# A selective scan in 64 units: two spread inflows, a shorter look-ahead for GpSimd, and a transposed output projection

## The reference

```
shift, scale, gate = split(silu(c) @ Wada.T + bada)
skip = ln(x) * (1 + scale) + shift          # then a second ln
act_mx = silu(Wx x_ssm + bx)
z_d = Wc_d (Wz x_ssm + bz) + bc_d           # d = 1 forward, d = 2 on the flipped sequence
delta, B, C = projections of z_d
h_t = exp(delta_t * A_n) * h_(t-1) + delta_t * B_t,n * z_t      # for each n of 16
y_t = sum_n h_t,n * C_t,n  (+ z_t * Dp)
out = Wf (act_mx*y1 + act_mx*y2) + bf + skip
return x + gate * out
```

## Time and profile before

| | us |
|---|---|
| median of 3 runs | 3407.84 (3405.9 to 3410.21) |
| profiled execution, its own time | 3410.34 |
| its span, first to last instruction | 3408.4 |
| mean granted TensorE clock | 0.965 of full |

### The profile page before, as it was taken

How to read it: one execution, slowest core, us unless ns; L and a number is a source line. 1 busy time by engine, 2 the same in 40 slices (tenths; PEclk the granted TensorE clock), 3 DMA queues, 4 the chain that set the end, 5 groups by cost and what they waited for, 6 DMA issues and landing times.

```text
span 3408.4 us, 49569 instructions
## 1 busy us (share of the span) xinstructions
PE 2982.9 (88%) x17232; PEld 2142.3 (63%) x17232; DVE 3090.2 (91%) x1983; ACT 2667.4 (78%) x5070; POOL 2982.0 (87%) x1352
## 2 busy tenths in 40 slices
PE   8987888898888888888888888898888888888898
PEld 3554666666666666666666666666666666666665
DVE  2546999999999999999999999999999999999995
ACT  0336898988788898987777898988777898987772
POOL 1335999999999999999999999999999999999996
PEclk9988999999999999999999999999999999999999
DMA  5575344744557344645457334645457344644463
GB/s 217 177 251 186 127 138 141 236 157 164 176 189 261 131 139 142 237 143 168 158 199 249 131 134 145 231 150 162 158 197 255 125 143 141 225 155 161 152 214 114
DMA packets 215920, 594.67 MB, mean 174 GB/s; under 512 B 21276, under 2 KB 67548, under 8 KB 211320
## 3 DMA queue, kind: packets, MB, share of 16 engines
q1 hardware_dynamic: 213224, 572.63, 49.7%
q0 software_dynamic: 2304, 16.78, 1.3%
q10 hardware_dynamic: 144, 2.10, 0.2%
HBM read 510.79 MB, written 80.63 MB: 174 GB/s over the span
## 4 chain that ended last, share of the span: by engine, by line
DVE 27%; PE 25%; POOL 21%; issue 17%; ACT 1%; DVEq 0%; POOLq 0%; ACTq 0%
POOL hbuf L1201 16%; DVE slot L1298 15%; DVE hbuf L1298 8%; PE y L868 7%; POOL bst L1196 5%; PE mb L950 4%; PE mb L839 3%; PE slot L879 3%; DVE hbuf L1303 2%; DVE delta L1240 2%; PE slot L890 2%; PE mb L849 1%; PE mb L941 1%; PE mb L909 1%; ACT abuf L1101 1%
## 5 line engine op out<-in xcount | busy, mean ns | idle before, releaser
L1201 POOL TENSOR_TENSOR hbuf<-hbuf,cres 128x1024 f32<-128x1024 f32 x640 | 1507.5, 2375 | 174.5 <-DVE hbuf L1298 173.7
L1196 POOL TENSOR_TENSOR bst<-bst,du 128x1024 f32<-128x1024 f32 x576 | 1359.3, 2376 | 62.5 <-DVE du L1250 60.9
L868 PE MATMUL y<-ident,hbuf 128*128 128x128 f32 x8192 | 1096.3, 282 | 86.7 <-POOL hbuf L1201 86.5
L868 PEld LDWEIGHTS y<-ident,hbuf 128*128 128x128 f32 x8192 | 968.5, 146 | 251.8 <-POOL hbuf L1201 165.3
L1298 DVE TENSOR_TENSOR_SCAN hbuf<-dec,slot 128x1024 f32<-128x1024 f32 x448 | 1019.5, 2276 | 80.9 <-PE slot L890 58.3
L1101 ACT ACTIVATE abuf<-dut,bt 128x128 f32<-128x128 f32 x3072 | 971.1, 387 | 0.0
L1298 DVE TENSOR_TENSOR_SCAN slot<-slot,bst 128x1024 f32<-128x1024 f32 x384 | 875.5, 2280 | 13.2 <-ACT slot L1160 12.6
L1160 ACT ACTIVATE slot<-delta,par 128x1024 f32<-128x1024 f32 x576 | 639.9, 1111 | 232.6 <-DVE hbuf L1303 212.7
L879 PE MATMUL slot<-ident,abuf 128*128 128x128 f32 x3072 | 426.1, 284 | 208.8 <-ACT abuf L1101 173.9
L1160 ACT ACTIVATE dec<-delta,par 128x1024 f32<-128x1024 f32 x448 | 510.9, 1140 | 96.0 <-DVE hbuf L1298 96.0
L879 PEld LDWEIGHTS slot<-ident,abuf 128*128 128x128 f32 x3072 | 356.4, 145 | 341.1 <-ACT abuf L1101 201.4
(11 more groups left out here) (152 smaller groups left out, 2207.1 us busy)
## 6 DMA issues: line engine op xcount, KB each, us to landing
bst<-bc_s SPq DMA_DIRECT2D x576, 512.0 KB, 3.8
cres<-bc_s SPq DMA_DIRECT2D x128, 512.0 KB, 7.0
wzs<-wz_s SPq DMA_DIRECT2D x64, 256.0 KB
yf_s<-yrd SPq DMA_DIRECT2D x32, 512.0 KB, 5.3
ybuf<-yf_s SPq DMA_DIRECT2D x32, 512.0 KB, 4.7
yg_s<-ybuf SPq DMA_DIRECT2D x31, 512.0 KB, 4.4
si_s<-silu SPq DMA_DIRECT2D x28, 512.0 KB, 6.0
silu<-si_s SPq DMA_DIRECT2D x28, 512.0 KB, 5.3
```

Source lines behind the costliest of these rows:

```text
L868: last = nc.tensor.matmul(y[:, j * P:(j + 1) * P], hbuf[:, q % HR, j * P:(j + 1) * P], ident[:], start=False, stop=(q % N == N - 1), is_tr ...
L1196: nc.gpsimd.tensor_tensor(bst[:, i % BR, :], bst[:, i % BR, :], du[:, k % 2, :], ALU.mult).then_inc(pool_b, 1)
L1201: nc.gpsimd.tensor_tensor(hbuf[:, q % HR, :], hbuf[:, q % HR, :], cres[:, q % N, :], ALU.mult).then_inc(pool_prod, 1)
```

## The change

- KINDS: chunk 1 becomes V, chunks 2 and 4 are E (before: E at 1, V at 2, A at 4). Six V, two E, five A, three P. A second diagonal tile, one made at c = 14, one at c = 0 of the next unit. Ten half steps of scaling a unit, where twelve were.
- The sums run four chunks behind (LAG), before three; HR = 5. `skip_terms` moves from c = 3 to c = 4, `copy_y` from c = 2 to c = 3.
- DR = 2 and BR = 4: GpSimd makes inflows two V/P chunks ahead, before three, and there are four B tiles.
- One `wz` tile, loaded at c = 0 for the next unit, before two tiles and two units ahead.
- The projection gives its block with channels on partitions: `project_tile` has the weights as the stationary operand, four matmuls of 128 columns for one of 512. `add_skip` adds the skip tile with four transposes on TensorE. DVE finishes the result with four scalar_tensor_tensor of 128x128 (times gate, plus x); GpSimd has no part in it any more. The gate is turned in the setup and stays in SBUF; x comes, and the output goes, in the turned layout.

```diff
-KINDS = "VEVVAVAPAVAPAPAV"
-SCALE_STEPS = {0: (4, 0), 2: (4, 1), 3: (6, 0), 5: (6, 1), 6: (8, 0), 7: (8, 1),
+KINDS = "VVEVEVAPAVAPAPAV"
+SCALE_STEPS = {3: (6, 0), 5: (6, 1), 6: (8, 0), 7: (8, 1),
                8: (10, 0), 9: (10, 1), 10: (12, 0), 11: (12, 1), 12: (14, 0), 13: (14, 1)}
-SPREAD = KINDS.index("E")
+SPREAD = [n for n in range(N) if KINDS[n] == "E"]
-HR = 4
-DR = 3
-BR = 5
+HR = 5
+LAG = 4
+DR = 2
+BR = 4
...
-                    if c == 0 and k + 2 < NU:
+                    if c == 0 and k + 1 < NU:
                         sp.wait_ge(z_mm, 2 * k + 2)
-                        load_weights(k + 2)
+                        load_wz(k + 1)
+                        if k + 2 < NU:
+                            load_wdt(k + 2)
...
+            def project_tile(bank, e, tokens):
+
+                for m in range(DT):
+                    nc.tensor.matmul(bank[:, m * P:(m + 1) * P], wf[:, e, m * P:(m + 1) * P], tokens,
+                                     start=(e == 0 and m == 0), stop=False, skip_group_check=True)
+
+            def add_skip(i, bank):
+                for m in range(DT):
+                    last = nc.tensor.matmul(bank[:, m * P:(m + 1) * P], skip_tile(i)[:, m * P:(m + 1) * P], ident[:],
+                                            start=False, stop=True, is_transpose=True, skip_group_check=True)
+                last.then_inc(proj_mm, 1)
...
-                    if c == 3:
-                        if k + 1 < NU:
-                            delta_product(k + 1)
+                    if c == 3 and k + 1 < NU:
+                        delta_product(k + 1)
+                    if c == LAG:
                         skip_terms(k)
-                    if q >= 3:
-                        sum_chunk(q - 3)
+                    if q >= LAG:
+                        sum_chunk(q - LAG)
...
-            make_diagonal(0)
+            for i in range(len(SPREAD)):
+                make_diagonal(0, i)
...
+                    if c == 0 and k > 0 and k % ET == 0:
+                        make_diagonal(k // ET, 1)
...
-                    if c == 2 and k > 0:
+                    if c == LAG - 1 and k > 0:
                         copy_y(k - 1)
...
-                    if c == 3 and k > 0 and projection_of(k - 1) is not None:
-                        finish_result(projection_of(k - 1))
-                    if c == 7 and k == NU - 1:
-                        finish_result(projection_of(k))
...
+            def finish_result(i, bank):
+                for m in range(DT):
+                    last = nc.vector.scalar_tensor_tensor(
+                        out=x_tile(i)[:, m * P:(m + 1) * P], in0=bank[:, m * P:(m + 1) * P],
+                        scalar=gate[:, m, i // ET:i // ET + 1], in1=x_tile(i)[:, m * P:(m + 1) * P],
+                        op0=ALU.mult, op1=ALU.add)
+                last.then_inc(proj_read, 1)
```

More of the change, by code:

```diff
@@ L117, in gain_round_trip @@
                 sp.dma_start(scratch["gs"], rows[:, 4:6, :]).then_inc(gs_out, 16)
-                sp.dma_start(scratch["gate"], rows[:, 6, :]).then_inc(gs_out, 16)
-                sp.wait_ge(gs_out, 32)
+                sp.wait_ge(gs_out, 16)
                 sp.dma_start(gs[:].rearrange("p b m d -> p (b m d)"),
@@ L444, in _ @@
                     pe.wait_ge(row_step, 5)
+                    for m in range(DT):
+                        last = nc.tensor.matmul(ps[6][:, m * B:(m + 1) * B], rows[:, 6, m * P:(m + 1) * P], ident[0:B, 0:B],
+                                                start=True, stop=True, is_transpose=True, skip_group_check=True)
+                    last.then_inc(gate_mm, 1)
                 if f == 0:
@@ L520, in ssm_kernel @@
         bt = sb("bt", [P, 2, ET, N])
-        diag = sb("diag", [P, ET, P])
+        diag = sb("diag", [P, len(SPREAD), ET, P])
         wf = sb("wf", [P, ET, D])
         wx = sb("wx", [P, D])
-        skip, xres, gateb = (sb(n, [P, D]) for n in ("skip", "xres", "gateb"))
+        skip, xres = (sb(n, [P, D]) for n in ("skip", "xres"))
+        gate = t["gate_sb"]
         y = ctx.enter_context(nc.psum_tensor("y", [P, S], fp32))
@@ L889, in spread_inflow @@
                 for j in range(ET):
-                    last = nc.tensor.matmul(slot[q % 2][:, j * P:(j + 1) * P], dut[:, j * P:(j + 1) * P], diag[:, j, :],
+                    last = nc.tensor.matmul(slot[q % 2][:, j * P:(j + 1) * P], dut[:, j * P:(j + 1) * P], diag[:, i, j, :],
                                             start=True, stop=True)
@@ L949, in project @@
                 for e in es:
-                    last = nc.tensor.matmul(bank, yp_tile(i)[:, e, :], wf[:, e, :], start=(e == 0), stop=(e == ET - 1))
+                    project_tile(bank, e, yp_tile(i)[:, e, :])
                 if ET - 1 in es:
-                    last.then_inc(proj_mm, 1)
+                    add_skip(i, bank)
             def project_last(i, es):
@@ L972, in project_last @@
                 for e in es:
-                    last = nc.tensor.matmul(tail_bank(i), gated_tile(e)[:, j * P:(j + 1) * P], wf[:, e, :],
-                                            start=(e == 0), stop=(e == ET - 1))
+                    project_tile(tail_bank(i), e, gated_tile(e)[:, j * P:(j + 1) * P])
                 if ET - 1 in es:
-                    last.then_inc(proj_mm, 1)
+                    pe.wait_ge(rest_in, 32 * ET)
+                    add_skip(i, tail_bank(i))
             pe.wait_ge(ones_ready, 1)
@@ L1036, in _ @@
                             project_last(i, (ET - 2,))
-            for q in range(NU * N - 3, NU * N):
+            for q in range(NU * N - LAG, NU * N):
                 sum_chunk(q)
@@ L1109, in copy_bt, with make_diagonal @@
                                      ACT.Copy).then_inc(bt_ready, 1)
[L1111 removed]
+            def make_diagonal(g, i):
+                n = SPREAD[i]
                 act.wait_ge(bt_ready, g + 1)
                 if g > 0:
[L1114 removed]
+                    act.wait_ge(turned, before("AE", (g * ET - 1) * N + n + 1))
                 for j in range(ET):
[L1116 to L1117 removed]
+                    last = nc.scalar.activation(diag[:, i, j, :], ident[:], ACT.Copy, scale=bt[:, g % 2, j, n:n + 1])
+                last.then_inc(diag_ready[i], 1)
             def copy_dut(k, h):
@@ L1121, in copy_dut @@
                 if k > 0:
-                    act.wait_ge(turned, before("AE", (k - 1) * N + SPREAD + 1))
+                    act.wait_ge(turned, before("AE", (k - 1) * N + SPREAD[-1] + 1))
                 if k > 0:
@@ L1397 @@
         t[name] = nc.dram_tensor(f"in_{name}", v.shape, mybir.dt.from_np(v.dtype), kind="ExternalInput").ap()
-    t["out"] = nc.dram_tensor("out_t", (NC, P, TB, D), fp32, kind="ExternalOutput").ap()
+    t["out"] = nc.dram_tensor("out_t", (B * ET, P, D), fp32, kind="ExternalOutput").ap()
     build(nc, t)
     got = run_bass_kernel_spmd(nc, [feed], core_ids=[0])
-    return np.ascontiguousarray(got.results[0]["out_t"].transpose(0, 2, 1, 3).reshape(B, S, D))
+    return np.ascontiguousarray(
+        got.results[0]["out_t"].reshape(B * ET, P, DT, P).transpose(0, 3, 2, 1).reshape(B, S, D))
```

94 lines of the change are left out of this document (40 added, 54 removed).

## The result

The changed kernel takes 3552.76 us (median of 4 runs, 3550.25 to 3553.4) against 3408.1 before: a ratio of 1.0423, 95% interval 1.0405 to 1.0441. It is slower, as forecast, but by 144.7 us and not by 104; the range ended at 3545.

A forecast was written before the change was run, and what follows sets the result against it. GpSimd's fixed order was taken to bound the changed kernel, 49.26 us a forward unit. Units +98.1, last boundary +1.0, start +2.4, tail +2.5 on 3410.3 gave 3514.3, less 2.5 for the median: 3512 us, range 3490 to 3545.

The forecast's parts named there:

- GpSimd's order decides: GpSimd's fixed order of inflows and products sets the pace: a forward unit takes 49.26 us against 46.99 before.
- The loop from P6 to I1': GpSimd's product of chunk 6 to next unit's chunk 1 inflow: 32.74 us from scan 6's start to scan 1's.
- The stall in units with projection: DVE at chunk 5 waits for ScalarE's late decays: 0.4 us, between 0 and 1, making the unit 50.18.
- The waits for the spread inflow: DVE's waits for TensorE's spread inflow, 1.95 us at scan 1 in projection units before, were to be near nothing.
- the 2.4 for the second diagonal: At the kernel's start, making a second diagonal on ScalarE before the first scan adds 2.4 us.
- the last boundary and the tail: End of the kernel: last unit boundary +1.0 us, final results at TensorE's pace +2.5, between 0 and 4.
- Four finishing instructions: DVE's four 128-column instructions finishing a projection: 1.16 us taken, bounds 0.48 and 2.7, replacing one of 0.58.
- TensorE's other work: Turned projection at equal cost, four added transposes 0.5 us, second spread about 1 us a unit: hidden behind the longer loop.
- ScalarE's chain: Rival: copy_y, Abs, Exp and chunk 5 decays come 1 us later than reckoned; +50 us, 3565 us, chance 10%.
- The rival with the faster outcome: GpSimd operations take 2.09 us instead of 2.325, its loop stays hidden and DVE bounds: 3341 us, chance 5%.

The follow-up runs named there:

- DR = 3: The changed kernel with only the constant DR set from 2 back to 3, four B tiles kept: 3366.82 us, ratio 0.9884 to the kernel before.
- the best version: The changed kernel with DR = 3 and, on TensorE at c = 3, the sum of chunk 15 ahead of delta_product: 3343.94 us, ratio 0.9811 to the kernel before.
- doubled spread: The changed kernel with the first spread inflow computed twice in units behind a projection, 16 matmul passes more: 3523.4 us.
- old kinds, DR = 3: The changed kernel with DR = 3 and the chunk kinds, single diagonal and twelve scaling half steps of before: 3405.19 us.

## Why the prediction was right, and where it fell short

*GpSimd's order decides: right.* The loop from P6 to I1' measured 32.81 against 32.74 worked out, forward units 49.3 where no other wait joins, units without silu or projection 48.7 against 48.62. Undoing one constant gave back 186 us (with the stall at chunk 4 gone as well), moving one inflow 62. The waits stand where they were put, 1.77 and 1.06 before chunks 0 and 1 (forecast 1.6 and 1.2). That DVE would idle, and GpSimd be no quicker for it, is right as well: its spacing stays at 2.33.

*The stall in units with projection: mis-sized.* This is the step that failed. I gave "a stall of 0.4, between 0 and 1", counted with delta_product at 1.8 and the sum at 1.0. These are times at full clock. In the changed kernel TensorE waits 2.8 us for the finish, and in 18 of 22 such units its clock falls just as its queue becomes critical: delta_product took up to 3.75 and the sum up to 1.92. A stall came at chunk 4, where none was forecast. In 14 units DVE waits there for the spread, some 0.86 us where the stretch at half clock was short and 2.4 to 2.5 where it was long; in 4 it waits some 1 us for ScalarE's decays, late for the same reason. Per unit 51.58 against 50.18: a stall of some 1.8 in the mean where 0.4 was taken, and 22 times 1.4 is 31 us. The waits for the spread inflow, forecast near nothing, came to 23.7 us, nearly all of it here. The 3 units with the wait in which the clock stayed took 50.08 to 50.28; with the clock kept up by added work the mean was 50.21. So the rest of the step's sum was right. I had read in the earlier trace rows that TensorE waited 1.36 us there before, and did not ask what a longer wait, which my own loop made certain, would do to its clock.

*Smaller terms.* Boundaries after silu units 49.49 against 49.26: +7.5 us; about every second one is some 0.4 longer, with a wait of 0.17 to 0.5 for ScalarE's decays at chunk 5. Unit 16 has a projection too, which I had counted among those without: 1.6. Outside these the errors nearly cancel, which is luck: the start was 0.2 later, not 2.4 (delta 0 came 2.5 earlier in this execution, 275.1 against 277.6; between the kernels here the start differs by a few us without a pattern that I can name; from delta 0 to delta 1 it was 33.85 and not 31.17, so the 2.4 for the second diagonal was about right); the last boundary and the tail 4.4, not 3.5. In all +40 in the units and -1 outside.

*Four finishing instructions.* 1.03 us from 1579.38 to the next scan at 1580.41, against 1.16 taken from the line through two rows. The estimate from the Trainium skill, VectorE: DVE Perf Modes, section on the TRN2 errata, was 1.03: the trace agrees with the page.

*TensorE's other work.* The turned projection and the second spread are hidden, as said; in the tail, which goes at TensorE's pace, each of the last results costs 7.58 us from start to start where it was 6.86 (3404.50 less 3397.64). The row of before, then two of after:

```profile
3397.64 0.69 DVE L1324 TENSOR_TENSOR cres<-mb,gateb 128x512 f32<-128x512 f32 x1 [5.45 <-PE mb L973]
...
3540.43 1.12 DVE L1284 SCALAR_TENSOR_TENSOR cres<-mb,gate_sb,cres 128x128 f32<-128x128 f32 x4 [6.46 <-PE mb L963]
3548.01 1.12 DVE L1284 SCALAR_TENSOR_TENSOR cres<-mb,gate_sb,cres 128x128 f32<-128x128 f32 x4 [6.46 <-PE mb L963]
```

*The rivals.* ScalarE's chain did not bind by itself, but it came in third place with 0.2 to 0.7 at chunk 5. With DR = 3 it was the main wait left inside the units (24 us); moving one sum removed the 15 of them that stood at chunk 5, and the 8 before chunk 15, once in eight units, stayed. The rival with the faster outcome did not come true: GpSimd's operations stayed at 2.33. But its size was right for a kernel in which the order no longer binds: 3341 was worked out for DVE as the bound, and the best version takes 3344.

## What to carry to other kernels

When queues work through fixed orders, don't compare busy shares: take one operation that waits for the other engine, count what stands behind it up to the next thing the other engine needs, and add the way back. That sum is a bound of the period that no idle elsewhere can lower, and a look-ahead constant enters it with whole operations. Once a new wait is certain, or an old one gets longer, ask every engine that waits longer because of it what it does next, and whether TensorE's clock will still be up when it goes on. And when a variant takes the same time as before, compare it by kind of unit: a gain and a loss can cancel.

## What the runs showed of the hardware

TensorE's clock fell to half around idles of 1.4 to 2.8 us, not every time, and more often where the idle was longer. Ahead of delta_product in units with projection, by kernel:

| kernel | usual idle, us | units in which the clock fell there |
|---|---|---|
| doubled spread; DR = 3 | 1.0 | 0 of 22 in either |
| kernel before | 1.36 | 4 of 22, no unit longer for it |
| old kinds, DR = 3 | 1.8 | 16 of 22 |
| changed kernel | 2.8 | 18 of 22 |

In the changed kernel delta_product then took up to 3.75 us in place of 1.95. Adding two microseconds of useless matmuls in front of the idle made the program 29 us faster. The Trainium skill, TensorE: Matmul & The Clock Gate, section on HAM oscillation, describes kernels that lose time in this way. In which units the clock falls, and for how long, these runs don't explain; the kernels also differ in what TensorE does before the idle. GpSimd's tensor_tensor of 128x1024 keeps its 2.33 us whether DVE beside it is busy or not.
